# Gathered w1 rows for the first layer of a spiking feed-forward block, with the idle row still added mostly by VectorE

## The chip, the cores and the metric

The kernel runs on one core of a Trainium2 chip. The metric is the device time of one launch in microseconds (us), as the median of several runs. Work is spread over TensorE (PE in the profile), VectorE (DVE), ScalarE (ACT), GpSimd (POOL), and the DMA engines, to which SyncE (SP) issues plain transfers and GpSimd issues indirect ones.

## The reference, cut to what matters

The input x has 2 batches of 2048 tokens with 512 channels. A channel adds up `relu(x) * 0.001` over the tokens on top of a start value below 1, and it spikes where the floor of that sum rises. The spikes, divided by 0.001, go through a feed-forward block with 2048 hidden units:

```python
c = initial_state[:, None, :] + cumsum(relu(inputs) * DT, axis=1)
fl = floor(c)
spikes = fl - prev                      # prev: fl one token earlier
h = relu((spikes / DT) @ w1 + b1)
out = x + (h @ w2 + b2)
```

With these inputs a channel spikes at most once. A count over the inputs of the reference gives 421 and 427 spiking channels in the two batches, on 386 and 380 tokens. Most of those tokens have one spike (353 and 340). The others, 33 and 40, have several, and 35 and 47 further channels spike on them. A token without a spike gets `x` plus one row that is the same for all of them, `relu(b1) @ w2 + b2`: the idle row.

## The kernel before, in words

**Idle row.** It is `relu(b1) @ w2 + b2`. VectorE adds up nine of its sixteen chunks by hand (`idle_by_hand`, `BY_HAND = 9`), TensorE the rest in four strips of 32 columns (`add_strips`, then `join_strips`). ScalarE copies it to `idle_row`. Then `add_idle(b, begin, end)` adds it to tokens `begin` to `end` of each of the 128 blocks of 16 tokens of batch b, in place in `x_sb`. A store of four token positions is 1.05 MB; there are four per batch, called here (b, 0) to (b, 3). SyncE issues them in one fixed order, each as soon as its own adds are done, and waits for them in that order:

```python
for b, q in ((0, 0), (0, 3), (0, 1), (0, 2), (1, 3), (1, 0), (1, 1), (1, 2)):
    store_idle(b, q)
```

VectorE adds (0, 0), then later (0, 1), (0, 2), (1, 0), (1, 1) with one instruction each (L673). GpSimd adds (0, 3), (1, 3) and (1, 2), one token position at a time (L354). It waits for values of the semaphore `reading_psum`, which VectorE raises.

**Table.** For a token with a single spike the whole output depends on the channel alone. TensorE computes a table with one row per channel: `relu(w1[channel] / DT + b1) - relu(b1)` (ScalarE, L422 and L423) times w2 (L807, 16 chunks of four parts each, a part being two matmul instructions). Its 64 parts are TensorE's work up to the first layer, and everything else that TensorE does is put between parts by hand.

**Finding the tokens.** VectorE sums x per block (`block_totals`), TensorE makes running sums of the blocks (`sum_totals`), VectorE finds the block in which each channel crosses 1 (`find_blocks`), GpSimd gathers these sixteen values per channel (L342), VectorE finds the token (`find_bases`, `find_tokens`). TensorE spreads the tokens over the partitions (`spread_tokens`), VectorE compares all channels with all (`count_met`, L600, four instructions per batch) and finds the first channel of each shared token (`find_leads`). TensorE numbers the leads (`count_leads`), VectorE makes a one-hot matrix of the numbers (`find_slots`, L617 and L619), and TensorE finds with it the token of each of 128 slots (`find_slots`, L879). All this is done for batch 0, then for batch 1.

**Shared tokens.** VectorE compares channels with slots (`first_spikes`, `second_spikes`), which gives the spikes of the up to 128 shared tokens, `spk_t`. `first_layer` (L888) is sixteen chunks of four matmuls of `w1_sb` with `spk_t` into two PSUM banks, ScalarE applies the relu (L452), `second_layer` (L895) is sixteen matmuls with w2. VectorE adds x and b2 (L727, L729: `new_row`), and GpSimd writes the rows (L381). That write waits for nothing but its rows and its place in GpSimd's queue.

**Single tokens.** GpSimd adds table rows to the stored output with four scatters per batch (L347). The four of a batch wait until all four stores of that batch have landed (`idle_stored`, L373). Between the two batches stands the gather of x for the shared tokens (L370). L381 comes after all eight.

**Guard.** If over 128 tokens are shared, or a channel could spike twice, everything is done again token by token (`redo`). With these inputs it isn't.

Of the kernel before, what the change touches and what calls it, by code (L numbers as in the profile page):

```python
# [18 lines left out]
def spike_ffn(nc, x, x_turned, cond, cond_cols, w1, w_pairs, b1_cols, b2, out):  # L19
# [5 lines left out]

    B, S, D = x.shape
# [10 lines left out]
    WQ = 4  # L37
# [5 lines left out]
    NOT_FIRST = 1024.0  # L43
    assert BLK == 16 and D == 512 and B == 2 and F == 2048
# [10 lines left out]
    with ExitStack() as ctx:  # L55
# [11 lines left out]
        w1_sb = sb("w1_sb", [P, DC, F])  # L67
# [10 lines left out]
        hot = sb("hot", [P, NE, P])  # L78
# [41 lines left out]
        leads = sb("leads", [P, NE])  # L120
        single = sb("single", [P, NE])
        leads_run = sb("leads_run", [P, NE])
        slot = sb("slot", [P, NE])
# [8 lines left out]
        checks = sb("checks", [P, 2])  # L132
        slot_row = sb("slot_row", [P, 1])
        slot_rows = sb("slot_rows", [P, B])
        diagonal = sb("diagonal", [P, P])
        crowd = sb("crowd", [P, 1])
# [8 lines left out]

        again = x_sb[0]
        own_x = again[:, 0, :]
# [22 lines left out]
        ps_slots = ps_met  # L170
        ps_hidden = [ps_turn, ps_small]
        ps_out = ps_table[0]
        ps_checks = ps_table[DC - 1]
# [4 lines left out]
        w1_in = [sem(f"w1_in{i}") for i in range(WQ)]  # L178
# [26 lines left out]
        met_counted = sem("met_counted")  # L205
        leads_ready = sem("leads_ready")
        leads_before = sem("leads_before")
        slot_ready = sem("slot_ready")
        hot_ready = sem("hot_ready")
        slots_found = sem("slots_found")  # L210
# [14 lines left out]
        spk_ready = sem("spk_ready")  # L225
# [37 lines left out]
        def _(sp):  # L263
# [47 lines left out]
        def _(pool):  # L311
# [23 lines left out]

            last_row = pool.to_reg(ROWS - 1)

# [47 lines left out]
            with pool.If(redo > 1):  # L385
                pool.wait_ge(singles_scattered, 16 * NE)
                pool.wait_ge(general_scattered, 16)
                pool.dma_start(own_init, cond.rearrange("(o b) d -> o b d", o=1).to_broadcast([P, B, D])).then_inc(
# [20 lines left out]
        def _(act):  # L409
# [35 lines left out]
            act.wait_ge(strips_summed, 1)  # L445
# [9 lines left out]
            for m in range(FC):  # L455
                relu_hidden(m, hidden_summed, m + 1, hidden_ready)
                if 1 <= m <= DC:
                    act.activation(table_row[m - 1], ps_table[m - 1][:, :], ACT.Copy).then_inc(table_rows_ready, 1)
# [17 lines left out]
        def _(dve):  # L476
# [115 lines left out]
            def count_met(b):  # L592
# [3 lines left out]
                if b == B - 1:  # L596
                    dve.sem_inc(reading_psum, 1)
# [395 lines left out]
```

## Time and profile before

| | us |
|---|---|
| median of 3 runs | 104.52 |
| lowest, highest | 104.49, 104.67 |
| the profiled execution | 103.89 |
| its span, first to last instruction | 102.1 |
| TensorE, VectorE, ScalarE, GpSimd busy | 95.4, 65.9, 35.5, 43.2 |
| mean granted TensorE clock | 0.991 |

The profiled execution gives all durations below. It is 0.63 us under the median, and its span is 1.79 us shorter than its time. Busy times are of the span; a TensorE that is always busy tells only that it had something in its pipeline.

### The profile page before, as it was taken

How to read it: one execution, taken by the hardware profiler on the slowest of the kernel's cores; microseconds unless marked ns; L12 is line 12 of the kernel's file. 1: busy time of each engine (PE TensorE's matmuls, PEld its weight loads, DVE VectorE, ACT ScalarE, POOL GpSimd, SP SyncE). 2: the span in 40 equal slices, each digit the busy share in tenths (PEclk: the TensorE clock that was granted, in tenths of full speed). 3: DMA queues.
4: the chain of work that ended last, by engine and by line, in shares of the span. 5: the costliest groups of instructions: out<-in, count | busy, mean ns of one | idle time of the engine just before them, and what ended most of it. 6: DMA issues, size and time to landing. Idle time of an engine off the chain costs nothing.

```text
span 102.1 us, 1157 instructions
## 1 busy us (share of the span) xinstructions
PE 95.4 (93%) x370; PEld 54.0 (53%) x370; DVE 65.9 (64%) x142; ACT 35.5 (35%) x64; POOL 43.2 (42%) x44
## 2 busy tenths in 40 slices
PE   5999999999999999999969999999999999999910
PEld 5944444444644444644234564649999984444300
DVE  2448999888699999488958888899993020020020
ACT  2796515315372540569740000003953330000000
POOL 6350000000078700017508181499937883688040
PEclk9999999999999999999999999999999999999996
DMA  1999999999999999999999725427999999998701
GB/s 58 286 387 414 417 420 411 411 407 409 409 409 409 396 393 401 409 394 387 379 373 352 324 116 218 193 125 292 395 430 436 407 336 195 218 115 106 92 8 62
DMA packets 10028, 31.66 MB, mean 310 GB/s; under 512 B 1671, under 2 KB 1799, under 8 KB 8994
## 3 DMA queue, kind: packets, MB, share of 16 engines
q1 hardware_dynamic: 8304, 29.63, 74.7%
q0 software_dynamic: 1568, 1.90, 11.4%
q8 instruction: 5, 0.08, 0.3%
q14 instruction: 5, 0.04, 0.1%
q10 hardware_dynamic: 146, 0.01, 0.1%
HBM read 21.58 MB, written 10.75 MB: 316 GB/s over the span
## 4 chain that ended last, share of the span: by engine, by line
PE 50%; DVE 20%; POOL 13%; issue 11%; ACT 1%; POOLq 1%; DVEq 0%
PE ps_table L807 40%; DVE x_sb L673 11%; POOL out L347 11%; PE ps_small L900 4%; DVE same L600 3%; PE ps_idle L823 2%; PE ps_turn L844 2%; DVE hot L619 1%; PE ps_idle L827 1%; PE ps_idle L833 1%; DVE spk_t L634 1%; POOL out L381 1%; POOL general_x L370 1%; POOLq L258 1%; DVE spk_t L629 1%
## 5 line engine op out<-in xcount | busy, mean ns | idle before, releaser
L807 PE MATMUL ps_table<-w_sb 128*128 128x512 f32 x128 | 56.9, 595 | 0.0
L807 PEld LDWEIGHTS ps_table<-w_sb 128*128 128x128 f32 x128 | 23.6, 190 | 27.1 <-issue 26.4
L342 POOL DMA_INDIRECT rates<-in_x_turned,sixteen_at x8 | 9.9, 1236 | 33.9 <-DVE sixteen_at L563 32.1
L354 POOL TENSOR_TENSOR x_sb<-x_sb,idle_row 128x512 f32<-128x512 f32 x12 | 14.9, 1277 | 9.9 <-DVEq L706 3.7
L422 ACT ACTIVATE w_sb<-w_sb,b_col 128x512 f32<-128x512 f32 (+2 forms) x19 | 12.2, 643 | 16.5 <-DMA w_sb<-in_w_pairs 16.3
L549 DVE SCALAR_TENSOR_TENSOR total_two<-x_sb,total_two 128x1024 f32<-128x1024 f32 x14 | 17.1, 1225 | 1.2 <-DMA x_sb<-in_x 0.8
L347 POOL DMA_INDIRECT out<-w_sb,to_single x8 | 12.5, 1558 | 5.8 <-issue 3.7
L895 PE MATMUL ps_table<-w_sb 128*128 128x512 f32 x32 | 14.0, 595 | 0.0
L423 ACT ACTIVATE w_sb<-w_sb,minus_relu_b 128x512 f32<-128x512 f32 (+2 forms) x19 | 12.3, 649 | 0.6
L673 DVE TENSOR_TENSOR x_sb<-x_sb,ps_idle 128x2048 f32<-128x2048 f32 x5 | 11.2, 2283 | 1.5 <-ACT idle_row L448 1.3
L895 PEld LDWEIGHTS ps_table<-w_sb 128*128 128x128 f32 x32 | 6.0, 190 | 7.2 <-issue 6.9
L452 ACT ACTIVATE w_sb<-ps_turn,b_col 128x128 f32<-128x128 f32 x8 | 2.9, 367 | 19.0 <-PE ps_turn L888 18.4
L888 PE MATMUL ps_small<-spk_t,w_sb 128*128 128x128 f32 x64 | 8.5, 275 | 0.0
L888 PE MATMUL ps_turn<-spk_t,w_sb 128*128 128x128 f32 x64 | 8.5, 275 | 0.0
L888 PEld LDWEIGHTS ps_turn<-spk_t,w_sb 128*128 128x128 f32 x64 | 7.9, 192 | 0.5 <-DVE spk_t L634 0.3
L888 PEld LDWEIGHTS ps_small<-spk_t,w_sb 128*128 128x128 f32 x64 | 7.8, 192 | 0.0
L509 DVE SCALAR_TENSOR_TENSOR idle_part<-w_sb,relu_b,idle_part 128x512 f32<-128x512 f32 x9 | 6.7, 750 | 1.5 <-DMA w_sb<-in_w_pairs 1.4
L729 DVE TENSOR_TENSOR w_sb<-ps_table,general_x 128x512 f32<-128x512 f32 x1 | 0.7, 692 | 6.3 <-PE ps_table L895 6.3
L900 PE MATMUL ps_small<-ones 128*128 128x128 f32 x16 | 3.7, 427 | 1.1 <-POOLq L320 1.1
L727 DVE TENSOR_TENSOR general_x<-general_x,b_row 128x512 f32<-128x512 f32 x1 | 0.7, 691 | 6.2 <-DMA general_x<-in_x,from_general 6.2
L900 PEld LDWEIGHTS ps_small<-ones 128*128 128x128 f32 x16 | 3.5, 330 | 1.1 <-POOLq L320 1.1
L665 DVE TENSOR_SCALAR crowd<-ps_table 128x1 f32<-128x1 f32 x1 | 0.2, 159 | 6.1 <-PE ps_table L871 6.1
(113 smaller groups left out, 65.5 us busy)
## 6 DMA issues: line engine op xcount, KB each, us to landing
x_sb<-in_x SPq DMA_DIRECT2D x16, 512.0 KB, 14.3
out<-x_sb SPq DMA_DIRECT2D x8, 1024.0 KB, 4.1
w_sb<-in_w_pairs SPq DMA_DIRECT2D x15, 512.0 KB, 15.7
w_sb<-in_w SPq DMA_DIRECT2D x4, 1024.0 KB, 15.3
w_sb<-in_w_pairs SPq DMA_DIRECT2D x2, 256.0 KB, 2.9
b_row<-in_b SPq DMA_DIRECT2D x1, 256.0 KB, 15.3
rates<-in_x_turned,sixteen_at POOLq DMA_INDIRECT x8, 6.5
out<-w_sb,to_single POOLq DMA_INDIRECT x8
```

The lines of the kernel that those rows point to most:

```text
L342: pool.indirect_dma_start(out=rates[:, col, :], out_offset=None, in_=x_sixteen, in_offset=bass.IndirectOffsetOnAxis(ap=sixteen_at[:, col:c ...
L347: pool.indirect_dma_start(out=out_rows, out_offset=bass.IndirectOffsetOnAxis(ap=to, axis=0), in_=row, in_offset=None, bounds_check=last_ro ...
L354: last = pool.tensor_tensor(x_sb[b][:, t, :], x_sb[b][:, t, :], idle_row[:, :], ALU.add)
L422: chain(act.activation(weights, weights, ACT.Relu, bias=b1_col[:, m:m + 1], scale=PER_DT))
L423: act.activation(weights, weights, ACT.Identity, bias=minus_relu_b1[:, m:m + 1]).then_inc(table_hidden_ready, 1)
L509: step = dve.scalar_tensor_tensor(out=idle_part[:, :], in0=w2_sb[:, m, :], scalar=relu_b1[:, m:m + 1], in1=idle_part[:, :], op0=ALU.mult, ...
L549: chain(dve.scalar_tensor_tensor(out=total_two[b][:, :, :], in0=tokens, scalar=0.0, in1=total_two[b][:, :, :], op0=ALU.max, op1=ALU.add))
L673: last = dve.tensor_tensor(tokens, tokens, along(ps_idle[:, :], end - begin), ALU.add)
L807: last = pe.matmul(ps_table[c][:, :], table_hidden[:, m, c * P:(c + 1) * P], w2_sb[:, m, :], start=(m == 0), stop=(m == FC - 1))
L888: last = pe.matmul(ps_hidden[m % 2][:, 0:P], w1_sb[:, c, m * P:(m + 1) * P], spk_t[:, c, :], start=(c == 0), stop=(c == DC - 1))
L895: last = pe.matmul(ps_out[:, :], hidden[m], w2_sb[:, m, :], start=(m == 0), stop=(m == FC - 1))
L900: pe.matmul(ps_small[:, 0:P], ones[:, :], ones[:, :], start=True, stop=True)
```

## The change

The first layer no longer multiplies all of w1 by a spike matrix. Two groups of channels are listed: group 0 holds for each slot the channel that leads its token, group 1 each further channel that spikes on a shared token, in slots of its own. The one-hot matrices are now per batch and group and in bf16. TensorE multiplies them with four small columns per channel (`named`: block, token in the block, and the channel's number in two parts). VectorE makes row numbers from that, and GpSimd gathers the w1 rows (8 KB each) of batch 0 and batch 1 into `spiking_rows[0]` and `spiking_rows[1]`; slots without a channel get a number past the end and are left out. The load of w1 goes away. The first layer is two matmuls per chunk: group 0 times the identity, group 1 times `others_turn`, which says to which token each row belongs. It writes three PSUM banks in turn.

Around it the order changes. `find_tokens(0)` goes ahead of `find_blocks(1)`, half of the strips and ScalarE's `idle_base` come earlier, and VectorE's first `add_idle` goes behind `find_leads(1)` in two halves. GpSimd adds token 12 of batch 0, then gathers, and then waits for the second value of `reading_psum`, which VectorE now gives after `turn_others`. The store (1, 2) is added by VectorE. ScalarE's copies of the table come after its sixteen relus, and `sum_checks` goes into the middle of the second layer. The order of the stores is as before.

```diff
-            for i in range(WQ):
-                part = slice(i * (F // WQ), (i + 1) * (F // WQ))
-                sp.dma_start(w1_sb[:, :, part], w1.rearrange("(c p) f -> p c f", p=P)[:, :, part]).then_inc(w1_in[i], 16)
...
+            for g in range(GROUPS):
+                pool.memset(spiking_rows[g][:, :], 0.0).then_inc(rows_cleared, 1)
...
+            def get_rows(b):
+                pool.wait_ge(rows_cleared, GROUPS)
+                for g in range(GROUPS):
+                    n = b * GROUPS + g
+                    pool.wait_ge(rows_listed, n + 1)
+                    if b > 0:
+                        pool.wait_ge(rows_got[g], 16 * b)
+                    pool.indirect_dma_start(out=spiking_rows[g][:, :], out_offset=None, in_=w1,
+                                            in_offset=bass.IndirectOffsetOnAxis(ap=row_at[:, n:n + 1], axis=0),
+                                            bounds_check=last_channel, oob_is_err=False).then_inc(rows_got[g], 16)
+
+            get_rows(0)
             pool.wait_ge(idle_copied, 1)
             pool.wait_ge(reading_psum, 1)
-            add_idle(0, 12, 14)
+            add_idle(0, 12, 13)
+            get_rows(1)
             pool.wait_ge(reading_psum, 2)
-            add_idle(0, 14, 16)
-            pool.wait_ge(reading_psum, 3)
+            add_idle(0, 13, 16)
             add_idle(1, 12, 16)
-            add_idle(1, 8, 12)
             pool.wait_ge(singles_listed, 1)
...
+            def list_rows(b):
+                for g in range(GROUPS):
+                    n = b * GROUPS + g
+                    dve.wait_ge(lists_found, n + 1)
+                    chain(dve.tensor_scalar(row_of[:, b, g, :], ps_list[g][:, b, 2:3], float(P), NO_ROW, ALU.mult, ALU.add))
+                    dve.tensor_tensor(row_at[:, n:n + 1], row_of[:, b, g, :], ps_list[g][:, b, 3:4], ALU.add).then_inc(
+                        rows_listed, 1)
...
+            find_tokens(0)
             find_blocks(1)
-            find_tokens(0)
+            count_met(0, 0, DC)
+            find_leads(0)
             find_bases(1)
-            count_met(0)
-            find_leads(0)
-            dve.wait_ge(idle_copied, 1)
-            dve.sem_inc(reading_psum, 1)
-            add_idle(0, 0, 4)
+            find_slots(0)
             find_tokens(1)
-            find_slots(0)
-            count_met(1)
+            list_rows(0)
+            count_met(1, 0, DC)
             find_leads(1)
-            first_spikes()
+            add_idle(0, 0, 2)
             find_slots(1)
+            add_idle(0, 2, 4)
+            list_rows(1)
+            find_row_tokens()
+            find_odd()
+            count_crowd()
+            turn_others()
             dve.sem_inc(reading_psum, 1)
             add_idle(0, 4, 8)
-            second_spikes()
             add_idle(0, 8, 12)
             add_idle(1, 0, 4)
             add_idle(1, 4, 8)
+            add_idle(1, 8, 12)
             list_singles()
...
+            def list_rows(b):
+                for g in range(GROUPS):
+                    pe.wait_ge(hot_ready, b * GROUPS + g + 1)
+                    for c in range(DC):
+                        last = pe.matmul(ps_list[g][:, b, :], hot[:, b, g, c, :], named[:, b, c, :],
+                                         start=(c == 0), stop=(c == DC - 1))
+                    last.then_inc(lists_found, 1)
...
+            def first_layer():
+                pe.wait_ge(rows_got[0], 16 * B)
+                pe.wait_ge(rows_got[1], 16 * B)
+                pe.wait_ge(others_ready, 1)
                 for m in range(FC):
+                    if m >= HB:
+                        pe.wait_ge(hidden_ready, m - HB + 1)
+                    chunk = slice(m * P, (m + 1) * P)
+                    pe.matmul(ps_hidden[m % HB][:, 0:P], spiking_rows[0][:, chunk], ident[:, :], start=True, stop=False)
+                    pe.matmul(ps_hidden[m % HB][:, 0:P], spiking_rows[1][:, chunk], others_turn[:, :],
+                              start=False, stop=True).then_inc(hidden_summed, 1)
...
             table_chunk(9)
-            table_part(10, 0, 3)
+            table_part(10, 0, 2)
             sum_totals(1)
-            table_part(10, 3, DC)
-            table_chunk(11)
+            table_part(10, 2, DC)
+            add_strips(0, 4)
             spread_tokens(0)
-            add_strips(0, FC - BY_HAND + 1)
+            table_part(11, 0, 3)
+            add_strips(4, FC - BY_HAND + 1)
+            table_part(11, 3, DC)
             table_part(12, 0, 1)
             join_strips()
-            table_part(12, 1, 3)
+            table_part(12, 1, 2)
             count_leads(0)
-            table_part(12, 3, DC)
-            table_part(13, 0, 3)
+            table_part(12, 2, DC)
+            list_rows(0)
+            table_part(13, 0, 2)
             spread_tokens(1)
-            table_part(13, 3, DC)
-            find_slots(0)
-            table_part(14, 0, 3)
+            table_part(13, 2, DC)
+            table_part(14, 0, 2)
             count_leads(1)
-            table_part(14, 3, DC)
-            table_part(15, 0, 1)
-            find_slots(1)
-            table_part(15, 1, DC)
+            table_part(14, 2, DC)
+            list_rows(1)
+            table_part(15, 0, 2)
+            spread_row_tokens()
+            table_part(15, 2, DC)
+            first_layer()
+            second_layer(ps_out, hidden_ready, 0).then_inc(out_summed, 1)
```

## Rows read from the trace of the kernel before

**Rows 1.** The page: span, DMA rate in 40 slices of 2.55 us, chain by engine.
```profile
span 102.1 us, 1157 instructions
GB/s 58 286 387 414 417 420 411 411 407 409 409 409 409 396 393 401 409 394 387 379 373 352 324 116 218 193 125 292 395 430 436 407 336 195 218 115 106 92 8 62
PE 50%; DVE 20%; POOL 13%; issue 11%; ACT 1%; POOLq 1%; DVEq 0%
```

**Rows 2.** Chain that ended last, in order of time: start, length, what.
```profile
26.34 16.31 PE ps_table L807 x38
...
93.09 1.55 POOL out L347
94.64 3.55 issue
98.42 1.03 POOL out L381
```

**Rows 3.** Timeline of the tail: start, length, engine, line, tiles [idle before <- releaser].
```profile
83.36 13.98 PE L895 MATMUL ps_table<-w_sb 128*128 128x512 f32 x32
...
87.52 1.56 POOL L347 DMA_INDIRECT out<-w_sb,to_single  x1 [2.06 <-DMA out<-x_sb]
...
97.45 0.69 DVE L729 TENSOR_TENSOR w_sb<-ps_table,general_x 128x512 f32<-128x512 f32 x1 [6.32 <-PE ps_table L895]
```

**Rows 4.** Timeline of SyncE's stores, 56 to 77 us, out of five windows.
```profile
56.21 0.36 SPq L301 DMA_DIRECT2D out<-x_sb  x1
61.72 0.36 SPq L301 DMA_DIRECT2D out<-x_sb  x1
67.46 0.33 SPq L301 DMA_DIRECT2D out<-x_sb  x1
70.69 2.66 SPq L301 DMA_DIRECT2D out<-x_sb  x2
75.09 1.63 SPq L301 DMA_DIRECT2D out<-x_sb  x2
```

**Rows 5.** Stretches: length, busy per engine, TensorE clock, DMA share, GB/s.
```profile
57.00:59.00 2.00, 2.00 (x9) 1.14 (x8) 1.63 (x6) 0.00 (x0) 0.00 (x0) 1.00 1.02 422
72.00:77.00 5.00, 5.00 (x47) 5.00 (x47) 4.76 (x16) 3.48 (x9) 3.08 (x4) 1.00 1.01 413
71.00:87.30 16.30, 16.30 (x122) 14.16 (x122) 6.79 (x22) 7.38 (x19) 11.32 (x9) 1.00 1.00 352
```

**Rows 6.** Timeline, first layer: chunks 1 and 2 and the relu of chunk 1.
```profile
69.82 1.06 PE L888 MATMUL ps_small<-spk_t,w_sb 128*128 128x128 f32 x8
70.71 1.06 PE L888 MATMUL ps_turn<-spk_t,w_sb 128*128 128x128 f32 x8
70.91 0.37 ACT L452 ACTIVATE w_sb<-ps_small,b_col 128x128 f32<-128x128 f32 x1 [0.53 <-PE ps_small L888]
```

**Rows 7.** Timeline of VectorE and TensorE, 41 to 53 us.
```profile
41.26 0.69 DVE L552 TENSOR_TENSOR total<-total_two 128x512 f32<-128x512 f32 x1
42.49 1.05 PE L844 MATMUL ps_turn<-up_to,total 128*128 128x128 f32 x8
43.59 0.69 DVE L559 TENSOR_TENSOR under<-ps_turn,theta_sum 128x512 f32<-128x512 f32 x1 [1.63 <-PE ps_turn L844]
45.22 0.19 DVE L582 TENSOR_SCALAR rates<-rates 128x64 f32<-128x64 f32 x1
46.85 0.17 DVE L569 SCALAR_TENSOR_TENSOR valid<-blocks_under,some 128x4 f32<-128x4 f32 x1
48.21 1.49 PE L823 MATMUL ps_idle<-w_sb,relu_b 128*32 128x512 f32 x11
48.77 0.75 DVE L600 SCALAR_TENSOR_TENSOR same<-ps_met,token,weigh 128x512 bf16<-128x512 f32 x1
50.06 0.70 PE L807 MATMUL ps_table<-w_sb 128*128 128x512 f32 x1
52.06 0.16 DVE L607 SCALAR_TENSOR_TENSOR is_first<-met,valid 128x4 f32<-128x4 f32 x1 [0.15 <-DVE same L600]
```

**Rows 8.** Groups by form: instructions x count, busy, mean ns, idle before.
```profile
L673 DVE TENSOR_TENSOR x_sb<-x_sb,ps_idle 128x2048 f32<-128x2048 f32 x5 | 11.2, 2283 | 1.5 <-ACT idle_row L448 1.3 <-DVE hot L619 0.2
L619 DVE TENSOR_TENSOR hot<-slot,slot_name 128x512 f32<-128x512 f32 x2 | 1.4, 691 | 0.1
L657 DVE TENSOR_TENSOR slot_row<-slot_rows 128x1 f32<-128x1 f32 x1 | 0.2, 160 | 0.0
L354 POOL TENSOR_TENSOR x_sb<-x_sb,idle_row 128x512 f32<-128x512 f32 x12 | 14.9, 1277 | 9.9 <-DVEq L706 3.7 <-DVEq L714 3.4 <-DVEq L597 2.7
```

**Rows 9.** The gathers of line L342: durations, and us from issue to landing.
```profile
L342 POOL DMA_INDIRECT rates<-in_x_turned,sixteen_at x8: 942/954/2003, 28.5 to 49.3; - x8
DMA to landing us min/median/max: 5.3/6.5/7.2
```

More of the change, by code:

```diff
@@ L36, in spike_ffn @@
     TH = BLK // XH
-    WQ = 4
     STRIP = 32
@@ L590, in find_tokens, with count_met @@
                 dve.sem_inc(token_ready, 1)
-            def count_met(b):
-                dve.wait_ge(token_spread, b + 1)
-                dve.wait_ge(const_ready, 7)
-                if b == B - 1:
-                    dve.sem_inc(reading_psum, 1)
-                for c in range(DC):
+            def count_met(b, begin, end):
+                if begin == 0:
+                    dve.wait_ge(token_spread, b + 1)
+                    dve.wait_ge(const_ready, 7)
+                    if b == B - 1:
+                        dve.sem_inc(reading_psum, 1)
+                for c in range(begin, end):
                     col = b * DC + c
@@ new lines, in find_slots @@
+                steps[0] += GROUPS
+                dve.wait_ge(dve_step, steps[0])
+                for g in range(GROUPS):
+                    dve.tensor_tensor(hot[:, b, g, :, :], over(slot[:, b, g, :], P), along(slot_name[:, :], DC),
+                                      ALU.is_equal).then_inc(hot_ready, 1)
+            def list_rows(b):
+                for g in range(GROUPS):
+                    n = b * GROUPS + g
[3 more added lines that the diff above has]
+                        rows_listed, 1)
@@ new lines, in find_row_tokens @@
+            def find_row_tokens():
+                for g in range(GROUPS):
+                    dve.tensor_copy(token_parts[:, g, :], ps_list[g][:, 0, 0:2]).then_inc(dve_step, 1)
+                steps[0] += GROUPS
+                dve.wait_ge(dve_step, steps[0])
+                for g in range(GROUPS):
+                    dve.tensor_tensor(token_parts[:, g, :], token_parts[:, g, :], ps_list[g][:, 1, 0:2],
+                                      ALU.add).then_inc(dve_step, 1)
+                steps[0] += GROUPS
+                dve.wait_ge(dve_step, steps[0])
+                chain(dve.scalar_tensor_tensor(out=row_token[:, :, :], in0=token_parts[:, :, 0:1], scalar=float(BLK),
+                                               in1=token_parts[:, :, 1:2], op0=ALU.mult, op1=ALU.add))
+                dve.sem_inc(row_tokens_ready, 1)
@@ L870, in sum_checks @@
                 pe.wait_ge(table_rows_ready, DC)
-                pe.matmul(ps_checks[:, 0:2], ones[:, :], checks[:, :], start=True, stop=True).then_inc(checks_summed, 1)
-            def find_slots(b):
-                pe.wait_ge(hot_ready, b + 1)
-                if b == 0:
-                    pe.wait_ge(met_counted, 1)
-                for c in range(DC):
-                    col = b * DC + c
-                    last = pe.matmul(ps_slots[:, b * P:(b + 1) * P], token[:, col:col + 1].to_broadcast([P, P]),
-                                     hot[:, col, :], start=(c == 0), stop=(c == DC - 1))
-                last.then_inc(slots_found, 1)
@@ L892, in second_layer @@
[L892 removed]
+                    last.then_inc(again_hidden_summed, 1)
+            def second_layer(to, ready, base):
                 for m in range(FC):
[L894 to L895 removed]
+                    if m == FC // 2 and to is ps_out:
+                        sum_checks()
+                    pe.wait_ge(ready, base + (max(m + 1, OUT_FREE) if to is ps_out else m + 1))
+                    last = pe.matmul(to[:, :], hidden[m], w2_sb[:, m, :], start=(m == 0), stop=(m == FC - 1))
```

172 lines of the change are left out of this document (90 added, 82 removed).

## The prediction

> **What bounds the kernel now.** I read the page first. TensorE has half of the chain, GpSimd 13% [rows 1]. Then the chain in order of time: up to 53 us it is TensorE's table, part after part without a gap, and it ends in GpSimd's scatters [rows 2]. The timeline of the tail shows that two paths come in close together. TensorE ends its second layer and VectorE makes `new_row` at 97.45; GpSimd issues the last write at 98.42, and the span ends 3.68 later [rows 2, 3]. GpSimd itself was free at 94.64. So the TensorE path sets the end, and the path of the scatters is 98.42 - 94.64 - 0.30 (the gap between two issues) = 3.5 us behind it.
>
> That second path is the one that I follow. Its scatters of batch 1 start at 87.52, released by a store of x_sb that had to land [rows 3]; landed at 87.52 - 0.23 = 87.29. The stores are 8 x 1.05 MB. Three were issued early, at 56.21, 61.72 and 67.46, and ran in gaps of other work; the last five were issued from 70.69 on and run back to back [rows 4]. In that time the DMA engines are full: 413 GB/s at a share of 1.01, as 422 with one store alone [rows 5]. From 70.69 to the landing are 16.6 us for 5.24 MB. At 413 GB/s these are 12.7 us, so 3.9 us are start, landing, and what batch 0's four scatters take from the stores (352 GB/s over the whole stretch).
>
> **The change: TensorE's tail.** A chunk of the first layer is 70.71 - 69.82 = 0.89 us for eight instructions [rows 6]; with two matmuls it is four, 0.445 us, so 16 chunks take 7.1 instead of 14.2. A relu is 0.37 us and starts 0.1 after its matmuls; with three banks it has 0.89, so it hides. The second layer is the same. What is new is that the first layer waits for the gathered rows, which I date below.
>
> **The change: loads.** w1 is 4.19 MB, about 10.5 us at some 400 GB/s. TensorE's table has no gap that waits for it [rows 2], so this gives the front nothing. DMA is simply done at about 45.5 instead of 56, and it then stands nearly idle, because no store is ready [rows 1, 4]. That is where a gain would have to come from, and the order of the adds decides it.
>
> **The change: the planning work.** It is one string through VectorE and TensorE. VectorE has the totals of batch 1 at 41.95 [rows 7]. `sum_totals(1)` is now a part (16.31 / 38 x 2 = 0.86 us [rows 2]) earlier in TensorE's queue and stands waiting for that, about 0.8 us, with the table behind it. `find_tokens(0)` takes 46.85 - 45.22 = 1.6 and fits into VectorE's old wait of 1.63 before L559; `find_blocks(1)` ends at 45.3 as before [rows 7].
> - TensorE from 43.3: two parts, 1.7; half of the strips, half of 50.06 - 48.21 = 0.9; the spread, 0.5. So `count_met(0)` starts at 46.6. Four compares and their reads take 52.06 - 48.77 = 3.3: to 49.9. `find_leads` 0.8, `find_bases(1)` (48.77 - 46.85, and one small operation more) 2.0: to 52.7.
> - TensorE meanwhile: three parts, 0.9 of strips, two parts, the join 0.9, one part, the count 0.3: 53.6. So `find_slots(0)` starts at 53.7. It has two small operations and two compares of 0.69 [rows 8]: 1.8, to 55.5. The bf16 matmuls with four columns are in no row. I take 0.45 us for eight, with 0 and the 0.89 of eight instructions of the first layer as bounds.
> - `find_tokens(1)` 57.1, `list_rows(0)` (four of 0.16, chained in pairs) 57.9. Spread of batch 1 at 58.2, `count_met(1)` to 61.6, `find_leads(1)` 62.4, half an `add_idle` (2.28 / 2 [rows 8]) 63.5, `find_slots(1)` 65.3, the other half 66.5, `list_rows(1)` 67.3. The first list of the two is ready at 66.9.
> - Seven small operations of `find_row_tokens` and the turn of them on TensorE, the checks, `turn_others`: 2.0 for thirteen short steps of 0.16 [rows 8], partly overlapped: 69.3. Only here does VectorE give the second `reading_psum`.
>
> Without any wait for TensorE the same list has 21.2 us behind 45.3: the second signal is at 66.5 at the earliest. With waits that I don't see I allow 71.
>
> **The change: GpSimd's queue.** `get_rows(1)` stands in GpSimd's queue between token 12 and token 13, so the adds of store (0, 3) wait behind two gathers. Their issue costs 0.94 to 2.00 us each, 1.24 on average [rows 9]; these were rows of 64 B, and 8 KB rows are in no row of the trace. With 1.24: 66.9 + 0.1 + 1.24 + 0.3 + 1.24 = 69.8, which is also past the signal. Then three adds at 1.25 (four tokens of (1, 3) and the rest follow): store (0, 3) can go out at 73.6, where it went out at 61.72 [rows 4]. The bounds are 70.3 (signal at 66.5, gathers hidden) and 76.6 (gathers at 2.00, and 1.5 of waits).
>
> **The change: the stores.** (0, 0) is added in two halves and goes out at 66.5 instead of 56.21. SyncE stays with its order, so (0, 1) and (0, 2), ready on VectorE at 71.6 and 73.9, can't pass (0, 3). Seven stores, 7.34 MB, are now behind 73.6, where five were behind 70.69. At 413 GB/s they take 17.8 us, and the same 3.9 for start, landing and batch 0's scatters (which come at about 83, inside the stretch): the last lands at 95.3. All later adds are ready in time: VectorE's five of 2.28 from 69.3 end at 80.8, GpSimd's (1, 3) at 78.7. This hides them, and `singles_listed` (81.4) and the table copies (first layer end and 2.4) too, because batch 0's stores land only at about 83.
>
> From the last landing GpSimd needs what it needed before: 94.64 - 87.29 = 7.35 for four scatters, 0.30, and 3.68 from the last write to the end: 106.6. The removed `add_idle(1, 8, 12)` takes 5.0 off GpSimd, but GpSimd is waiting there, so that is worth nothing.
>
> **TensorE's path now.** The second gather of batch 1 is issued at 68.5. It is about 0.35 MB of rows. Landings were 5.3 to 7.2 with full queues [rows 9]; I take 4 for emptier ones: 72.5. The table ends at 70.1 (stalls of 0.8, 0.4, 0.7, 0.9 and 0.6 against 1.8 of slot matmuls gone), so the first layer runs 72.5 to 79.7, and the second, 14.0 [rows 3], with the check in it, to 93.8. `new_row` is there at 94.6, 3.6 earlier than before, and waits 9 us in front of a GpSimd that is still scattering.
>
> **Sum.** Span 106.6 against 102.1: +4.5 us. The profiled execution would be 103.89 + 4.5 = 108.4; it lies 0.63 under the median of 104.52, so the median is 104.52 + 4.5 = 109.0.
>
> The Trainium skill ("DMA: Bandwidth & Descriptors", section "Where 436 GB/s comes from") says that transfers between HBM and SBUF are bound by HBM's share per core, about 358 GB/s. This case's trace has 413 and 422 with stores [rows 5], so here the rule is too low; by it the seven stores would take 20.5 us, and an estimate from that page would be 2.7 us later than mine.
>
> **Rivals.**
> - *A, the forecast:* the stores start late and end late, 109.0. For it: five stores and four scatters fill a full 16.6 us now [rows 4, 5], and two more are added behind a later start.
> - *B, faster: TensorE's path still decides.* The end is then `new_row` 3.6 us earlier, the median 100.9. It is so if the last store lands before 94.6 - 7.35 = 87.3; the turn from faster to slower is at 87.29 + 3.5 = 90.8. With seven stores at 413 GB/s and the 3.9, that needs (0, 3) out by 69.1, or the 3.9 gone and my earliest bound of 70.3 reached, which gives 70.3 + 17.8 = 88.1. For it: four scatters may cost less beside the stores than I charge, and DMA has 20 us with little to do. Against it: nothing in the order of adds lets a store into that time but (0, 0).
> - *C, slower still: the gathers cost GpSimd more.* A row of 8 KB may need several descriptors. At 2.5 to 3 us of issue each, (0, 3) goes out 2.5 to 3.5 later, and the median is about 112.
> - *D, the guard acts.* If a group held more than 128 rows, the kernel would redo everything token by token, for hundreds of us. The counts are 73 and 82, so I give it nothing.
>
> **Chances.** A 0.68, C 0.17, B and what lies between it and no change 0.12, within 0.2% of before 0.03. (0.2% is about what a measurement of this kernel can tell from no change.) Slower is A and C, 0.85. A alone has 106.5 to 111: its start bounds of 70.3 and 76.6 would make 105.7 to 112.0, but both ends need all costs on one side. The range for 8 in 10 takes in half of C and the low bound of A: 105.4 to 111.9.
>
> **What would show it.** Right: the second `add_idle` group of GpSimd starts at about 70; SyncE's store (0, 3) is issued at about 73.6; from there to about 92 the DMA share is near 1 at 400 GB/s; the first scatter of batch 1 starts at about 95.5; the first layer takes about 7.2 us, and L381's successor follows the last scatter with no gap. Wrong: DMA busy before 70 with more than one store, a first scatter of batch 1 before 91, or a wait for `new_row` at the end. A first layer that starts after 80 would be a different mistake, since TensorE would then be back on the path.

## The result, and the profile after

The changed kernel takes 110.25 us in the median (109.21 to 110.41, 4 runs). The kernel before takes 104.5 on the same chip. The ratio is 1.054, with a 95% interval of 1.046 to 1.062: slower, as forecast (109.0, range 105.4 to 111.9). The profiled execution took 110.37, with a span of 108.5, where the steps of the forecast gave 106.6.

From the page of the changed kernel, in the order of [rows 1]: span, granted clock and DMA rate in 40 slices of 2.71 us, and the chain by engine.

```profile
span 108.5 us, 1054 instructions
PEclk9999999999999999999999999996559999999985
GB/s 87 258 359 412 415 421 412 408 409 408 411 409 396 393 390 411 298 14 6 6 0 0 61 136 9 338 187 224 405 411 426 411 414 423 221 182 163 98 123 33
DVE 39%; PE 24%; POOL 11%; DMA 11%; issue 7%; POOLq 2%; ACT 1%; SPq 1%; DVEq 0%
```

In [rows 1] DMA is full up to about 56 us, has stores in the gap after it, and is full again from 70. Now the load ends near 46, and the 20 us behind that are nearly empty. The freed DMA time isn't used. TensorE's share of the chain is half of what it was. VectorE's has doubled, and most of that is its front: the block sums (16% of the span) and its chunks of the idle row (6%), because the planning string starts from these sums.

The timeline of SyncE's stores, from 67 us on, answers to [rows 4]:

```profile
67.58 0.35 SPq L317 DMA_DIRECT2D out<-x_sb  x1
74.66 2.50 SPq L317 DMA_DIRECT2D out<-x_sb  x3
79.57 1.77 SPq L317 DMA_DIRECT2D out<-x_sb  x2
```

Before, three of the eight stores were issued by 67.46. Now one is out at 67.58, and the second, (0, 3), at 74.66; the other six follow it. The timeline of GpSimd shows why, between the planning and the scatters (in brackets the idle time before an instruction, and what ended it):

```profile
68.58 1.00 POOL L386 DMA_INDIRECT spiking_rows<-in_w,row_at  x1 [5.64 <-DVE row_at L679]
69.88 1.00 POOL L386 DMA_INDIRECT spiking_rows<-in_w,row_at  x1 [0.31 <-issue]
70.91 8.63 POOL L374 TENSOR_TENSOR x_sb<-x_sb,idle_row 128x512 f32<-128x512 f32 x7
87.53 1.60 POOL L367 DMA_INDIRECT out<-w_sb,to_single  x1 [7.99 <-ACT w_sb L493]
...
94.99 1.01 POOL L402 DMA_INDIRECT general_x<-in_x,from_general  x1 [0.30 <-issue]
96.30 1.56 POOL L367 DMA_INDIRECT out<-w_sb,to_single  x1 [0.31 <-issue]
...
103.80 1.03 POOL L413 DMA_INDIRECT out<-w_sb,to_general  x1 [0.30 <-issue]
```

GpSimd stands idle for 5.64 us, until the list of rows is there, with three adds of (0, 3) queued behind the gathers. They need the second `reading_psum` too, which VectorE gives after `turn_others`, between 70.15 and 70.74, so both conditions end close together, the gathers' issue last (70.88). The third add ends 3.7 us after 70.91, and (0, 3) goes out. So far it is the forecast. Lower down it is not: batch 1's first scatter (96.30) has no wait for a store ahead of it. The string before it starts at 87.53, released by ScalarE's table copies. The chain of waits tells how those came to be late:

```profile
69.88 6.09 DMA spiking_rows<-in_w,row_at
76.06 0.77 PE ps_turn L959 x2
...
86.18 0.98 ACT w_sb L493 x2
87.53 1.60 POOL out L367
```

The same stretch by windows (length, busy time of each engine, granted clock, DMA share, GB/s), and the start of the first layer in TensorE's timeline:

```profile
70.00:76.00 6.00, 0.81 (x2) 0.00 (x0) 5.41 (x4) 0.00 (x0) 5.97 (x6) 0.84 0.66 225
76.00:81.00 5.00, 4.94 (x23) 4.97 (x24) 5.00 (x3) 1.77 (x5) 3.55 (x3) 0.51 1.02 416
81.00:86.00 5.00, 5.00 (x44) 4.80 (x43) 1.52 (x7) 3.93 (x12) 0.00 (x0) 1.00 1.01 415
```
```profile
76.06 0.77 PE L959 MATMUL ps_turn<-ident,spiking_rows 128*128 128x128 f32 x2 [5.25 <-DMA spiking_rows<-in_w,row_at]
76.62 0.63 PE L960 MATMUL ps_turn<-others_turn,spiking_rows 128*128 128x128 f32 x2
...
81.36 0.39 PE L960 MATMUL ps_turn<-others_turn,spiking_rows 128*128 128x128 f32 x2
```

TensorE waits 5.25 us for the rows. In that time its granted clock falls to half (1.2 of 2.4 GHz), and it stays there until 81: 23 matmuls in 5 us, then 44 in the next 5. The first layer takes from 76.06 to 85.8, 9.7 us instead of the 7.2 that I forecast. TensorE ends its second layer at 99.73, and `new_row` starts at 100.26: VectorE first adds b2 to the rows of x (99.54), which GpSimd gathers only at 94.99.

### The profile page after: what moved, and what is told of

It is laid out like the page before. It is cut to its first block, busy times and chain, and to the rows that moved or that the text cites. A ratio compares the mean times of both kernels' runs of the same rounds, so it can differ in the third digit from the quotient of the medians.

```text
span 108.5 us, 1054 instructions
## 1 busy us (share of the span) xinstructions
PE 91.6 (84%) x307; PEld 47.6 (44%) x307; DVE 71.7 (66%) x167; ACT 35.5 (33%) x64; POOL 44.7 (41%) x46
## 4 chain that ended last, share of the span: by engine, by line
DVE 39%; PE 24%; POOL 11%; DMA 11%; issue 7%; POOLq 2%; ACT 1%; SPq 1%; DVEq 0%
DVE total_two L590 16%; PE ps_table L872 10%; POOL out L367 8%; DMA spiking_rows<-in_w,row_at 6%; DVE idle_part L546 6%; DMA w_sb<-in_w_pairs 5%; DVE same L644 3%; DVE x_sb L736 2%; PE ps_turn L959 2%; POOLq L59 2%; PE ps_idle L888 2%; DVE start_t L557 2%; PE ps_turn L960 2%; PE ps_met L960 1%; PE ps_met L959 1%
## 5 line engine op out<-in xcount | busy, mean ns | idle before, releaser
L872 PE MATMUL ps_table<-w_sb 128*128 128x512 f32 x128 | 58.0, 601 | 0.0
L872 PEld LDWEIGHTS ps_table<-w_sb 128*128 128x128 f32 x128 | 23.8, 193 | 26.5 <-issue 25.0
L977 PE MATMUL ps_met<-w_sb 128*128 128x512 f32 x32 | 14.1, 595 | 0.0
L736 DVE TENSOR_TENSOR x_sb<-x_sb,ps_idle 128x2048 f32<-128x2048 f32 (+1 forms) x7 | 13.5, 1978 | 0.7 <-DVE others_turn L699 0.6
L374 POOL TENSOR_TENSOR x_sb<-x_sb,idle_row 128x512 f32<-128x512 f32 x8 | 9.9, 1269 | 0.1
L386 POOL DMA_INDIRECT spiking_rows<-in_w,row_at x4 | 4.0, 1005 | 14.4 <-DVE row_at L679 13.7
L977 PEld LDWEIGHTS ps_met<-w_sb 128*128 128x128 f32 x32 | 5.9, 190 | 6.7 <-issue 6.7
L959 PE MATMUL ps_turn<-ident,spiking_rows 128*128 128x128 f32 x12 | 2.9, 335 | 5.2 <-DMA spiking_rows<-in_w,row_at 5.2
L644 DVE SCALAR_TENSOR_TENSOR same<-ps_met,token,weigh 128x512 bf16<-128x512 f32 x4 | 3.0, 751 | 1.3 <-PE ps_met L921 1.2
L353 POOL MEMSET spiking_rows<- 128x2048 f32 x2 | 3.5, 1797 | 0.0
```

Source lines behind the costliest of these rows:

```text
L374: last = pool.tensor_tensor(x_sb[b][:, t, :], x_sb[b][:, t, :], idle_row[:, :], ALU.add)
L736: last = dve.tensor_tensor(tokens, tokens, along(ps_idle[:, :], end - begin), ALU.add)
L872: last = pe.matmul(ps_table[c][:, :], table_hidden[:, m, c * P:(c + 1) * P], w2_sb[:, m, :], start=(m == 0), stop=(m == FC - 1))
L959: pe.matmul(ps_hidden[m % HB][:, 0:P], spiking_rows[0][:, chunk], ident[:, :], start=True, stop=False)
L977: last = pe.matmul(to[:, :], hidden[m], w2_sb[:, m, :], start=(m == 0), stop=(m == FC - 1))
```

## The experiments

Two theories stood against each other from here. **S:** the stores set the end; they land at about 96 whatever TensorE does. **G:** the string of GpSimd from the table copies on sets it (87.53 + four scatters, a gather and their gaps = 96.30). In this trace both give the same time. Ratios are to the kernel before on the same chip. e1 to e4 ran on one chip, where it took 103.65, e5 to e8 on a second (103.46), and e9 to e11 on a third (103.55). The changed kernel itself did not run on the chip of e1 to e4. Its ratio was 1.054 on one chip and 1.068 on another (e5), so ratios that differ by less than that do not separate e1, e3 and e4 from it; there the times in the traces decide.

**e1, the table copies ahead of the relus**

```
+            act.wait_ge(table_summed, FC)
+            for c in range(DC):
+                act.activation(table_row[c], ps_table[c][:, :], ACT.Copy).then_inc(table_rows_ready, 1)
             for m in range(FC):
                 relu_hidden(m, hidden_summed, m + 1, hidden_ready)
-            for c in range(DC):
-                act.activation(table_row[c], ...)
```

> Against the changed kernel at 110.25 us. ScalarE copies the table rows as soon as the table is summed (about 70.9 us), ahead of the relus, instead of at 86 to 88. Theory G (the table copies behind a slow first layer release the first scatter at 87.5, and nine indirect DMAs then follow in one string without a wait): the first scatter starts when batch 0's stores have landed, at about 84; batch 1's scatters meet the landing of its stores at about 94.5, which they did not before, so only 1.5 to 2 of the 3.5 us are kept: 108.5, range 107.8 to 109.3. Theory S (my recorded one: the landing of batch 1's stores sets the string's second half, the copies are hidden): no change, 110.0 to 110.5.

It took 110.09, 1.062 (1.059 to 1.065). In the timeline of GpSimd:

```profile
86.22 1.60 POOL L367 DMA_INDIRECT out<-w_sb,to_single  x1 [6.72 <-issue]
...
93.67 1.01 POOL L402 DMA_INDIRECT general_x<-in_x,from_general  x1 [0.30 <-issue]
96.21 1.56 POOL L367 DMA_INDIRECT out<-w_sb,to_single  x1 [1.52 <-DMA out<-x_sb]
```

The first scatter comes 1.3 us earlier, and the string then stands 1.52 us for a store. The end hardly moves (the last write is issued at 103.62 instead of 103.80). So the stores land at 96.0, a bound of their own, as S says. The copies had come to lie upon it, and in the changed kernel either of the two would hold the end at nearly the same time. The gain at the first scatter is 1.3 and not 3.5, since batch 0's stores landed at about 86.0 and not at 84: the list of singles and the copies were there by 82.3, and nothing else was left to wait for.

**e2, the adds of tokens 12 to 16 ahead of batch 1's gathers**

```
-            add_idle(0, 12, 13)
+            add_idle(0, 12, 16)
             get_rows(1)
             pool.wait_ge(reading_psum, 2)
-            add_idle(0, 13, 16)
```

> Against the changed kernel at 110.25 us. GpSimd adds all four tokens of store (0, 3) ahead of the second batch's two gathers, so that store goes out about 7 us earlier, at 67.6 behind (0, 0). Theory S (stores decide): the stores end 2.6 us or more earlier and so does the kernel: 107 to 107.8. Theory G (table copies release the scatters): nothing is gained, 110 to 110.5; if the gathers now share the DMA engines with two stores instead of one, their rows land up to 2.6 us later and the kernel is slower by that: up to 112.8.

It took 116.95, 1.128 (1.123 to 1.133), beyond every theory. Store (0, 3) did go out 3.1 us earlier, at 71.56, but (0, 0) went out at 71.17 instead of 67.58, and the plan broke. VectorE's timeline at 61 to 67 us, and then GpSimd's and the start of the first layer in TensorE's:

```profile
61.64 0.75 DVE L643 SCALAR_TENSOR_TENSOR same<-ps_turn,token,weigh 128x512 bf16<-128x512 f32 x1
62.43 4.13 DVE L650 SCALAR_TENSOR_TENSOR is_first<-met,valid 128x4 f32<-128x4 f32 x1
66.59 0.16 DVE L652 TENSOR_TENSOR leads<-valid,is_first 128x4 f32<-128x4 f32 x1
```
```profile
61.62 4.91 POOL L374 TENSOR_TENSOR x_sb<-x_sb,idle_row 128x512 f32<-128x512 f32 x4
72.44 0.99 POOL L386 DMA_INDIRECT spiking_rows<-in_w,row_at  x1 [5.92 <-issue]
73.74 1.00 POOL L386 DMA_INDIRECT spiking_rows<-in_w,row_at  x1 [0.30 <-issue]
```
```profile
82.52 0.77 PE L958 MATMUL ps_turn<-ident,spiking_rows 128*128 128x128 f32 x2 [7.47 <-issue]
```

A step on four columns takes 4.13 us instead of 0.16: it ends when GpSimd's run of four adds does, while a compare that reads one operand from PSUM keeps its 0.75 beside the same adds. The gathers were issued at 72.44 and 73.74 instead of 68.58 and 69.88, 3.9 later, and the last one landed 8.7 us after its issue instead of 6.1, beside the two stores that had just gone out. This second part, 2.6 us, is what theory G had for gathers that share the DMA engines with two stores. The first part was in no theory. TensorE was idle for 7.47 us and ran the first layer from 82.5, 6.5 later, for 5.7 us of it at half clock. So the adds can't simply be moved into the planning. (In the kernel before they start together with VectorE's instructions that read an operand from PSUM: at 53.96 and 65.14 beside its own adds, which keep their 2.29 us, and at 59.20 beside the compares, which keep their 0.75.)

**e3, TensorE kept busy while it waits**

```
             spread_row_tokens()
             table_part(15, 2, DC)
+            for _ in range(22):
+                pe.matmul(ps_turn[:, 0:P], ones[:, :], ones[:, :], start=True, stop=True)
```

> Against the changed kernel at 110.25 us. 22 extra matmuls of ones (4.9 us) stand between the end of the table and the first layer, in the time in which TensorE waits for the rows. Theory G with the clock as its cause: TensorE's granted clock stays at 1.0 instead of 0.5 from 74 to 81, the first layer takes 7.2 instead of 9.7 us, the table copies end 2.5 earlier, and the string of scatters starts at about 85; batch 1's scatters may then wait a little for stores: 108.0 to 108.5. Theory S: the clock changes nothing at the end, 110.0 to 110.5.

It took 110.36, 1.063 (1.058 to 1.068). Windows of this kernel, and its GpSimd:

```profile
70.00:77.00 7.00, 6.24 (x49) 5.54 (x48) 6.35 (x4) 0.00 (x0) 6.83 (x6) 1.00 0.70 242
77.00:85.00 8.00, 8.00 (x67) 7.52 (x67) 5.78 (x9) 6.35 (x18) 2.85 (x3) 1.00 1.03 424
```
```profile
85.89 1.60 POOL L367 DMA_INDIRECT out<-w_sb,to_single  x1 [6.05 <-ACT w_sb L493]
...
96.78 1.56 POOL L367 DMA_INDIRECT out<-w_sb,to_single  x1 [2.42 <-DMA out<-x_sb]
```

The clock stays at 1.00 and the first layer is back at 7.2 us, so the idle time was what cost it its clock. The first scatter comes 1.6 earlier. Batch 1's waits 2.42 for the stores all the same, and nothing is gained: S again.

**e4, `spiking_rows` cleared later**

```
+            pool.wait_ge(clear_rows, 1)
             for g in range(GROUPS):
                 pool.memset(spiking_rows[g][:, :], 0.0).then_inc(rows_cleared, 1)
             ...
             block_totals(0, 0, 2)
+            dve.sem_inc(clear_rows, 1)
```

> Against the changed kernel at 110.25 us. GpSimd's two memsets of spiking_rows start only after VectorE's first two block sums (about 13.5 us in this order) instead of at 6.4. Theory M (the memsets hold up one small VectorE copy, 1.94 instead of 0.17 us, and everything that VectorE plans is about 1 us later for that): the totals of batch 1 are back at 41.3 instead of 42.2, and the kernel is 0.8 to 1.0 faster: 109.3. Rival (VectorE's lateness comes from the landing of w_pairs, 7.2 instead of 6.5, or is given back later in a wait for a transfer): below 0.3 us, 110.0 to 110.4.

It took 109.88, 1.058 (1.054 to 1.062). VectorE's timeline in the changed kernel, and then in e4:

```profile
8.06 1.94 DVE L557 COPY start_t<-start_c 128x16 f32<-128x16 f32 x1
```
```profile
7.30 0.17 DVE L559 COPY start_t<-start_c 128x16 f32<-128x16 f32 x1
```

The stall is real and goes: the copy waits out the memsets, which end at 9.97. But batch 1's totals are there at 42.03 instead of 42.22, and (0, 3) goes out at 74.47 instead of 74.66. The stall is not what makes the planning late.

**e5, the changed kernel again,** unedited, as the base for the second chip.

> The changed kernel, unedited, on the chip of the next three, so that they can be compared with it. Its ratio to the kernel before was 1.054 on the first chip, and the kernel before took 103.65 on the second. Every theory: ratio 1.05 to 1.06, so 109.2 to 110.2.

It took 110.12, 1.068 (1.062 to 1.074): the time is in the expected range, the ratio above it.

**e6, e1 without the stores (0, 2) and (1, 2)**

```
-            for b, q in ((0, 0), (0, 3), (0, 1), (0, 2), (1, 3), (1, 0), (1, 1), (1, 2)):
+            for b, q in ((0, 0), (0, 3), (0, 1), (1, 3), (1, 0), (1, 1)):
-            ... idle_stored[b], 16 * XQ
+            ... idle_stored[b], 16 * (XQ - 1)
```

> The kernel with early table copies (110.1), and the stores (0, 2) and (1, 2) left out, so that 2.1 MB of the output are never written; all adds are still made. Theory S (two bounds lie on each other at 96.2 us: the string of scatters from the table copies, and the landing of batch 1's stores; with early copies only the stores are left): batch 0's stores land 2.6 earlier, at 83.6, batch 1's 5.2 earlier, at 91.0, and the string from 83.6 reaches batch 1 at 92.4, so 3.8 are gained: 106.3, range 105.5 to 107. Theory W (the scatters wait for GpSimd's own adds or for the singles' list, both done by 82.5, and the stores only look like the cause): within 0.5 of 110.

It took 107.07, 1.037 (1.032 to 1.041), 3.1 us less than e5 and just above the range of S. GpSimd:

```profile
92.65 1.56 POOL L367 DMA_INDIRECT out<-w_sb,to_single  x1 [0.30 <-issue]
...
100.53 1.03 POOL L413 DMA_INDIRECT out<-w_sb,to_general  x1 [0.77 <-DVE w_sb L796]
```

Batch 1's scatters start 3.2 earlier than in e5 (95.84), without a wait. Then a new bound comes in, which S did not have: the last write waits 0.77 us for `new_row`. W is out, and the landing of the stores is a bound. The run also shows the next path close behind: even with a quarter of the stores gone, the kernel is slower than before.

**e7, the adds put into the gaps**, with e1 and e4

```
+            dve.wait_ge(idle_copied, 1)
+            dve.sem_inc(reading_psum, 1)
+            add_idle(0, 0, 4)
             find_slots(0)
             ...
-            add_idle(0, 0, 2)
-            add_idle(0, 2, 4)
```

On GpSimd tokens 12 and 13 stand beside that add, 14 beside the second `count_met`, and 15 behind the gathers.

> Early table copies and late memsets; VectorE adds all of (0, 0) ahead of find_slots(0), where it stood idle, GpSimd adds tokens 12 and 13 beside it, 14 beside count_met(1) and 15 behind the gathers. (0, 0) goes out at about 57, (0, 3) at about 72 instead of 74.6. Theory S: the seven stores behind (0, 3) start and end 2.7 earlier: 107.3, range 106.5 to 108.2. Theory L (what decides is the planning string; 2.3 us of adds earlier in it just move its waits): rows are gathered at the same time and the kernel stays at 109.5 to 110.2.

It took 109.78, 1.064 (1.058 to 1.069): S's range was missed, and the time lies in that of L. (0, 0) went out at 55.92 instead of 67.58, and (0, 3) at 72.94. From windows of e5 and then of e7:

```profile
72.00:76.00 4.00, 0.30 (x1) 0.33 (x2) 4.00 (x3) 0.00 (x0) 4.00 (x5) 0.70 0.59 236
```
```profile
72.00:76.00 4.00, 0.00 (x0) 0.00 (x0) 4.00 (x3) 2.04 (x4) 4.00 (x4) 0.98 0.86 307
```

(0, 3) ran beside the gathered rows, where DMA had been idle for two fifths. That is worth (0.86 - 0.59) x 4 = 1.1 us of DMA. Batch 1's first scatter came only 0.5 earlier than in e5 (95.37), after a wait of 2.08 for a store, so it is the stores that it waits for and not L's planning string. These 0.5 were lost again behind the last write, which has 5.2 us to the end of the span where e5 has 4.4. My step that the stores behind (0, 3) "start and end 2.7 earlier" is too simple: what counts is how many bytes are left once DMA is full for good. By the same account moving (0, 0) from 67.6 to 55.9 could change nothing; it fitted into idle time either way. That account is my reading, and e7 alone doesn't show it; e8 puts it to the test.

**e8, as e7, with (0, 1) added in the planning too**, token 15 beside it, and 22 matmuls of ones ahead of the first layer

```
+            dve.sem_inc(reading_psum, 1)
+            add_idle(0, 4, 8)
             find_slots(1)
             ...
+            for _ in range(22):
+                pe.matmul(ps_turn[:, 0:P], ones[:, :], ones[:, :], start=True, stop=True)
             first_layer()
```

> As the kernel before it, and (0, 1) is added behind find_leads(1), token 15 beside it, and 22 matmuls of ones keep TensorE busy while the rows land. (0, 3) and (0, 1) go out at about 66.5, five stores are behind 75.3. The planning string is 2.3 us longer, so the rows land at about 78 and new_row is there at 99.8, still ahead of the scatters. Theory S: the last store lands at 91.9, 105.9 in all, range 104.8 to 107. Theory L: the longer planning string is paid in full, 109 to 112.

It took 106.4, 1.030 (1.024 to 1.036), a time as expected. Two stores go out together at 67.01, so three are out by then, as in [rows 4]. The timeline of its GpSimd:

```profile
91.39 1.56 POOL L369 DMA_INDIRECT out<-w_sb,to_single  x1 [0.30 <-issue]
...
100.67 1.03 POOL L418 DMA_INDIRECT out<-w_sb,to_general  x1 [2.17 <-DVE w_sb L804]
```

Batch 1's scatters wait for no store any more, and the last write waits 2.17 for `new_row`, which VectorE starts at 99.70. I had expected that row to be there ahead of the scatters, so the time was right and the bound was not. The add in the planning made the list of rows late (gathers at 70.63 and 71.94), so TensorE is the bound. It is 3.7 us less than e5, and still behind the kernel before, where `new_row` starts at 97.45 [rows 3].

**e11, between the two:** half of that add in the planning, half behind it, `list_singles` earlier, 20 matmuls of ones.

> The best version so far (ratio 1.030), with (0, 1) added half in the planning string and half behind it, the singles listed earlier, and 20 matmuls of ones instead of 22. Both paths should meet: rows 1.1 us earlier, new_row at about 99.2, six stores behind 72.7 that land at 91.9. Theory S: about 1 us faster than 106.4, 105.3, range 104.7 to 106.2, still slower than the kernel before. If store time can't be bought back so late: 106.4 or more.

It took 107.23, 1.029 (1.020 to 1.038): missed, and within its interval no better than e8. GpSimd:

```profile
93.44 1.56 POOL L369 DMA_INDIRECT out<-w_sb,to_single  x1 [2.32 <-DMA out<-x_sb]
...
100.86 1.03 POOL L418 DMA_INDIRECT out<-w_sb,to_general  x1 [0.31 <-issue]
```

`new_row` starts 1.3 earlier (98.42), and the stores land at least 2 us later (93.2, where e8's first scatter of batch 1 started at 91.39 without a wait). The two paths trade against each other through VectorE's string, and the end comes no earlier.

**e9, the kernel before without three quarters of the w1 load.** It loads a quarter and reads it four times over in the first layer.

```
-            for i in range(WQ):
+            for i in range(1):
                 ... w1_in[i]
-                                 w1_sb[:, c, m * P:(m + 1) * P],
+                                 w1_sb[:, c, m % 4 * P:(m % 4 + 1) * P],
```

> The kernel BEFORE, with a quarter of w1 loaded (1.05 MB instead of 4.19) and that quarter used for all sixteen chunks, so 3.1 MB of loads are gone and the hidden values are not the reference's. My prediction said that the removed load gives nothing by itself, since the table has no gap that waits for it and no store is ready before 56: ratio to before 0.998 to 1.002. Rival: the transfers of stores, scatters or gathers after 56 were slowed by w1: 0.3 to 1 us faster, 0.990 to 0.997.

It took 103.9, 1.004 (0.9998 to 1.008), slightly above my range and clear of the rival's. Taking away 3.1 MB of load gives nothing, as forecast under "loads".

**e10, the kernel before with two of the four matmuls of each first-layer chunk**

```
-                    for c in range(DC):
+                    for c in range(2):
                         ... start=(c == 0), stop=(c == 1)
```

> The kernel BEFORE, with two of the four matmuls of each chunk of the first layer left out: the same number of TensorE instructions there as in the changed kernel, and nothing else of it. This is the gain on TensorE by itself. Theory S (a second path, the landing of the stores and the string of scatters, lies 3.5 us behind TensorE's): new_row is 5.4 to 7.1 earlier, but the last write can go out only at 94.9 instead of 98.4, and it lands about 1 us slower behind a scatter: 2.5 to 3.5 us faster, ratio 0.966 to 0.976. Rival (TensorE alone sets the end): all of it, 5.4 to 7.1 us, 0.93 to 0.95.

It took 101.14, 0.981 (0.972 to 0.990). The expected range was 0.966 to 0.976, so the gain is at its low end or below. GpSimd:

```profile
86.59 1.56 POOL L347 DMA_INDIRECT out<-w_sb,to_single  x1 [1.66 <-DMA out<-x_sb]
...
94.02 1.03 POOL L381 DMA_INDIRECT out<-w_sb,to_general  x1 [0.30 <-issue]
```

`new_row` is made 4.7 us earlier, at 92.76, and not 5.4 to 7.1: with the two banks of this kernel TensorE waits for the relus, and the first layer takes 9.7 us (68.80 to 78.5), a chunk 0.61 and not 0.445. The last write then stands directly behind the scatters, with 4.98 us from it to the end of the span (99.0) instead of 3.68. So the shorter first layer by itself is worth some 2 us (1 to 2.9 by the interval) before the stores' path stops it, and a still faster one would be worth no more, since the last write has no wait left. With the stores as they were, that is all that it could have brought. The changed kernel gets none of it: its stores land about 9 us later than before, and its rows come too late for an earlier `new_row`.

## Why the prediction was right

**The direction and the mechanism.** The forecast was case A: adds that stand behind the gathers let the stores out late, and the stores land late. e1 and e3 show the stores as a bound of their own at 96.0 and 96.5, e6 and e8 move the end by taking bytes out of the last full stretch, and e9 and e10 confirm the worth of the removed load (none) and of the shorter first layer (about 2, not 7). In the changed kernel the stores did not hold the end alone: the string from the table copies reached batch 1 at 96.30, 0.1 us behind what the stores allowed in e1.

**The terms.**
- (0, 3) out at 73.6 forecast, 74.66 measured. The planning ran about 1.0 late from its start on (batch 1's totals at 42.22 instead of 41.26), before anything of the new planning. The list was ready at 67.81 instead of 66.9, and the first gather started 0.8 behind it (68.58) where I had 0.1. The gathers' issue was 1.00 each and not 1.24, which gave 0.5 back: 0.9 + 0.7 - 0.5 = 1.1.
- From (0, 3) to the last landing: 21.7 forecast, 96.0 - 74.59 = 21.4 in e1. So the stream at 413 GB/s and the 3.9 for start, landing and scatters held as a sum; the window 76 to 81 has 416 at a share of 1.02. The 3.9 by itself is not measured, and batch 0's scatters came at 86.2 (e1) or 87.5 and not at 83. Here and in [rows 5] the trace lies above the 358 GB/s that the Trainium skill gives ("DMA: Bandwidth & Descriptors", "Where 436 GB/s comes from").
- Batch 1's first scatter at 95.5 forecast, 96.30 measured: +0.8. From there to the last write 7.50 instead of 7.42.
- From the last write to the end: 3.68 forecast, 108.5 - 103.80 = 4.7 measured, +1.0. In [rows 2] that write starts 3.8 us behind the last scatter's end on GpSimd, here 0.3. e10, with the same order in the kernel before, has 4.98. The landing of that write itself took 2.7 us in the kernel before, 3.5 in the changed one and 4.0 in e10. So the write lands later where it follows the scatters directly, and I had carried over a tail from a trace in which it had room. That their traffic is what it waits for is likely, and not shown.
- The sum of these: 106.6 + 0.8 + 0.1 + 1.0 = 108.5, the span measured. The median is only 1.25 above the forecast, since I had added 0.63 for a profiled execution below the median, and this one was not: that the forecast median is nearer than the forecast span (1.9 off) is luck.

**Steps that failed without moving the end.**
- "This hides them, and `singles_listed` [...] and the table copies [...] too". The copies released the first scatter at 87.53 and lay on the bound; that they pushed the end out by no more than 0.1 us is luck. The landing of the rows took 6.1 and not 4 (the last gather issued at 69.88), TensorE lost its clock while it waited, and the first layer took 9.7 and not 7.2. I read the clock nowhere in the prediction, though the change puts an idle stretch right ahead of a TensorE stage. `new_row` starts at 100.26 and is there at 100.95 instead of 94.6; its slack before the last write was 2.8 us, not 9 (8.4 by the forecast's own dates).
- The memsets of `spiking_rows` had no term at all. VectorE's copy beside them takes 1.94 us instead of 0.17 (e4 takes that away). What e2 met is the same sort of thing at a larger size, and the changed kernel has it too, beside its one add of token 12: `is_first` takes 0.49 there. The Trainium skill has the rule ("SBUF — State Buffer", "Who interferes with whom"): a VectorE copy in a two-port mode, or an operation with two inputs in SBUF against a GpSimd operation that reads SBUF, excludes GpSimd and is excluded by it. The traces agree: `is_first` 4.13 us instead of 0.16 beside the adds, the compare with an input in PSUM 0.75 as ever, and the copy held by the memsets. The page has the pair held "for the whole instruction"; here VectorE stayed out for four adds in a row. By that rule e2 would have been costed at a loss, of at most the adds' own 4.9 us, and not at a gain.

**Left open.** Of the 1.0 us by which the planning starts late, e4 explains 0.2. TensorE is 0.85 later at `sum_totals(0)` even in the changed kernel's e4 form (26.14 instead of 25.29), having waited some 0.5 in its first parts for ScalarE, and ScalarE starts on one chunk of `w_pairs`, when its load lands, at 23.82 instead of 23.25. I have not found why. Nor do I know why the gathers of rows start 0.8 us behind their list, where a gather of [rows 9] started 0.3 behind its own (45.58 against 45.30). And no run tells the two conditions on the adds of (0, 3) apart, the gathers ahead of them in the queue and the second signal. Nor did any order that I tried beat the kernel before: the best `new_row` with the list of rows in front of it started at 98.42 (e11), against 97.45 [rows 3].

## What to carry to other kernels

Removed traffic is worth something only where the work that is to use the free time is ready then. Here DMA stood idle for 20 us, and the stores that could have filled it were held by adds which stood in a queue behind the new gathers, and behind a signal that came only after the planning. A shortened stage is worth at most the distance to the next path (2 us in e10, where `new_row` came 4.7 earlier), and inputs that a plan must first find cost that plan, the landing and the clock that TensorE loses meanwhile. When a full stream of transfers sets the end, count the bytes that are left when it becomes full, not the moment at which the first of them starts.

## What the runs showed of the hardware

- A gather of 33 to 47 rows of 8 KB cost GpSimd 1.00 us of issue, no more than one of 64 B rows (0.94 to 2.00 in [rows 9]). It landed 4.5 to 6.1 us after issue in the changed kernel, and up to 8.7 us after it beside two stores (e2). A scatter that accumulates costs about 1.55, and 0.30 lie between two.
- An indirect write directly behind such scatters needs 4.4 to 5.2 us to the end of the span (4.4 in e5, 4.7 in the changed kernel, 5.0 in e10, 5.2 in e7); with 3.8 us of room it needed 3.68.
- After 5.25 us without work TensorE's granted clock was 0.51 for the next 5 us of work; with small matmuls in the gap it stayed at 1.00 (e3).
- VectorE can be shut out by GpSimd for several instructions on end: beside four adds of about 1.25 us one step of 0.16 us, with both inputs in SBUF, took 4.13 (e2). Steps with an input in PSUM kept their time.
